# Early root and pre-scaled residual for the last two images, and 64x64 tile products for the first two, in a four-image kernel on one core

## The chip, the cores and the metric

The kernel runs on one core of a Trainium2 chip. The metric is the device time of one execution in microseconds (us); less is better. The core has a matrix engine (TensorE, PE in the tables), a vector engine (VectorE, DVE), a scalar engine (ScalarE, ACT), GpSimd (POOL) and a DMA queue engine (SyncE, SP). Every engine works through its own list of instructions in order and waits on semaphores for the others.

## The reference

Four images of 256 channels and 32x32 pixels pass through four blocks, each of the form x + block(group norm of x). Cut to what the change touches:

```python
def _gn(v, G=32, eps=1e-05): ...            # group norm over 8 channels and all pixels
x = x + _L0(_gn(x), ...)                     # spatial attention, 8 heads
x = x + _L1(_gn(x), ...)                     # selective scan in 4 groups of 64 channels
x = x + _L2(_gn(x), ...)                     # channel attention
x = x + _L3(_gn(x), ...)                     # x + blend of two of seven max pools

# in _L1, for each group g of 64 channels:
dBu = delta * u * Bm                         # Bm: a row of x_dbl = xp_w @ u, spread over the group
h = scan(dA, dBu);  y = h * Cm + Ds * u      # Cm: another such row
y = layernorm(y, og, ob);  out = op_w @ (y * z)
# in _L2:
x_norm = (xt - mean) * rsqrt(var + EPS)      # xt: pixels x channels; one root for each pixel
q, k, v = qkv_w @ x_norm;  attn = softmax(q @ k^T)      # 32 x 32 for each of 8 heads
out = proj_w @ (attn @ v) + proj_b
```

Weights of the scan that belong to one group (`Bm`, `Cm`, `op_w`) are kept on the diagonal of 128x128 matrices, two groups in one, with zeros beside.

## The kernel before

The 256 channels are two chunks of 128 partitions (`cc` or `m`), the 1024 pixels two halves of 512, since a bank of PSUM holds 512 numbers of 4 bytes for each partition. Each image is cut into streams: F (first norm, queries, keys), A (spatial attention), C (its projection, the norm, the convolution of the scan block), B (the scan), D (channel attention), M (max pools of images 0 and 1, summed on VectorE), L and W (max pools of images 2 and 3, summed on TensorE). Every stream is a generator that yields after each step. Four strings (`PE_ORDER`, `ACT_ORDER`, `DVE_ORDER`, `SP_ORDER`) say how many steps of which stream come next on an engine, so the order over the four images is written out by hand; other strings (`BANKS_...`) say in which of eight PSUM banks each step's result lies. A step waits for the steps that it needs and for the last reader of its bank.

Names: `XRES[b % 2]` (XR in the rows) holds the residual x of an image; `U` the input of the scan; `XB`, `XC`, `OPW` the block-diagonal weights for Bm, Cm and op_w; `PVR` the inverse roots of the 1024 pixels as 128x8 numbers; `RB` its copy spread 32 times (in `T1`), `R` the root as one row of 1024 on all partitions, which lies in `HB`; `WE` (in `BUF`) is proj_w, attn and the value weights as one 256x256 matrix, scaled by the group norm; `GM` its means, `CST` = WE @ GM; `BE` the bias; `PA_` is the padded image that the pools read, `QST` the other pool buffer from image 2 on.

Block B on VectorE: `scan` multiplies by Bm from PSUM (L1278, steps dbu), scans (L1284), multiplies by Cm (L1290, steps hc); `gated` multiplies the product with op_w by the gate and the input (L1311, steps xm). On TensorE these are `by_chunk` (L1841) and `gated` (L1876): one 128x128 product of 512 columns for each half.

Block D at its end, for every image: when `WE` is there, TensorE makes `cst`, spreads the root (`spread_rows`, L1976: R0, R1), and multiplies WE with the residual in four products (`project`, L1665: out_m_half). ScalarE copies the root into `R`. VectorE makes two passes over each of the four results (`block3_out`):

```python
dst = (out - CST) * R          # L1396, steps x3a
dst = dst + BE + XRES          # L1401, steps x3, with a running sum for the next norm
```

`dst` lies in `PA_`, so this waits until the pools of the image before have been read. The root goes into `HB`, so its spreading waits for the last pool step of the image before (p6_1). Then come the max pools: L1464 to L1483 for the window of 3, and for each wider window one step along the row (L1495) and one along the column (L1500). For images 2 and 3 TensorE adds the pools (L2075, steps acc0 to acc6); each waits for its pool.

## Time and profile before

| what | value |
|---|---|
| median of 3 runs | 740.16 us (739.38 to 746.61) |
| profiled execution | 742.38 us |
| span in its trace, first to last instruction | 740.5 us |
| TensorE busy | 634.9 us (86%) |
| VectorE busy | 545.4 us (74%) |
| ScalarE busy | 417.8 us (56%) |
| granted TensorE clock, mean | 0.917 |

The profiled execution takes 1.9 us more than its span, which is the work before the first and after the last instruction. Shares are means over the whole span: which engine is full changes along it.

### The profile page before, as it was taken

What the parts mean: (1) busy time and instruction counts of PE and PEld (TensorE: products, weight loads), DVE (VectorE), ACT (ScalarE), POOL (GpSimd) and SP (SyncE); (2) the same over time, 40 slices, a digit from 0 to 9 for tenths busy, and PEclk for the clock granted to TensorE, in tenths of its full rate; (3) what the DMA queues carried; (4) which work ended last, traced back from release to release, by engine and by line L of the source; (5) the groups of instructions that cost most, each with busy time, mean ns of one, the idle gap of its engine ahead of it and who ended that gap; (6) DMA issues with size and microseconds to landing.
All of it is one profiled execution on the core that took longest, in us unless ns stands there. A gap on an engine that the chain in (4) does not pass through costs nothing.

```text
span 740.5 us, 9520 instructions
## 1 busy us (share of the span) xinstructions
PE 634.9 (86%) x3472; PEld 303.2 (41%) x3472; DVE 545.4 (74%) x995; ACT 417.8 (56%) x703; POOL 35.5 (5%) x26
## 2 busy tenths in 40 slices
PE   4769996798999979999998897999759659699687
PEld 3545442343333346353543462344315215465332
DVE  3477249523747466857789899987899998999696
ACT  1304644559778658664866795684667754442321
POOL 3300001000002000000030000100020000000000
PEclk9978997799999997999999988999879969899879
DMA  9240141001001220001000400011000001000101
GB/s 322 86 121 2 58 135 29 3 1 28 31 1 57 58 51 2 2 1 58 0 1 1 107 2 1 1 58 57 0 1 1 1 0 58 0 1 1 57 1 57
DMA packets 15855, 26.88 MB, mean 36 GB/s; under 512 B 3601, under 2 KB 7345, under 8 KB 15682
## 3 DMA queue, kind: packets, MB, share of 16 engines
q1 hardware_dynamic: 12512, 22.80, 10.1%
q10 hardware_dynamic: 3298, 3.48, 1.6%
q8 instruction: 28, 0.46, 0.3%
q14 instruction: 17, 0.14, 0.1%
HBM read 14.09 MB, written 4.19 MB: 25 GB/s over the span
## 4 chain that ended last, share of the span: by engine, by line
PE 62%; DVE 19%; ACT 12%; issue 4%; DMA 1%; ACTq 1%; SPq 0%; DVEq 0%
PE PSB L1665 14%; PE PSB L1795 9%; PE PSB L1776 6%; PE PSB L1686 4%; PE PSB L2075 4%; PE PSB L1699 3%; PE PSB L1809 3%; PE PSB L1741 3%; DVE NEGMAX L1185 3%; PE PSB L1761 3%; PE PSB L1909 2%; PE PSB L1876 2%; PE PSB L1841 2%; ACT PT L656 2%; ACT PS L753 2%
## 5 line engine op out<-in xcount | busy, mean ns | idle before, releaser
L1185 DVE TENSOR_REDUCE NEGMAX<-PSB 128x2 f32<-128x512 f32 x128 | 79.5, 681 | 22.8 <-PE PSB L1741 22.6
L656 ACT ACTIVATE PT<-PSB 128x512 f32<-128x512 f32 x128 | 67.4, 606 | 49.2 <-PE PSB L1761 49.0
L1795 PE MATMUL PSB<-XNP,WTAP 64*64 64x512 f32 x576 | 66.8, 616 | 2.6 <-issue 2.6
L1741 PE MATMUL PSB<-KST,QST 96*128 96x256 f16 x256 | 43.4, 320 | 10.8 <-DMA KST<-KL 7.7
L1761 PE MATMUL PSB<-QST,KST 98*128 98x512 f16 x128 | 38.8, 423 | 7.3 <-DMA QST<-ML 6.0
L1795 PEld LDWEIGHTS PSB<-XNP,WTAP 64*64 64x64 f32 x576 | 22.4, 139 | 45.3 <-issue 45.2
L1500 DVE TENSOR_TENSOR PA_<-HB 128x1024 f32<-128x1024 f32 x32 | 39.1, 1223 | 1.3 <-PE PSB L2075 0.6
L987 POOL TENSOR_TENSOR GA<-GA,PT 128x1024 f32<-128x1024 f32 x8 | 20.2, 2540 | 400.2 <-ACT PT L684 400.2
L1741 PEld LDWEIGHTS PSB<-KST,QST 96*128 96x128 f16 x256 | 25.7, 112 | 30.6 <-DMA KST<-KL 8.2
L720 ACT ACTIVATE U<-PSB 64x512 f32<-64x512 f32 x32 | 26.5, 829 | 20.5 <-PE PSB L1795 19.9
L1776 PE MATMUL PSB<-PT,VT 128*32 128x512 f32 x256 | 35.7, 630 | 1.8 <-issue 0.6
L2075 PE MATMUL PSB<-PA_,PT 128*128 128x512 f32 x64 | 33.2, 660 | 4.3 <-ACT PT L915 3.0
L1776 PE MATMUL PSB<-PT,ONES 128*32 128x512 f32 x256 | 34.4, 607 | 0.0
L1495 DVE TENSOR_TENSOR HB<-PA_ 128x1024 f32<-128x1024 f32 x28 | 34.1, 1219 | 0.2
L1699 PE MATMUL PSB<-XF,WDS 128*128 128x256 f32 x128 | 31.3, 403 | 3.1 <-DVE XF L1100 3.1
L1509 DVE SCALAR_TENSOR_TENSOR ACC<-PA_,COEF,ACC 128x1024 f32<-128x1024 f32 x24 | 32.9, 1371 | 0.4
L1164 DVE SCALAR_TENSOR_TENSOR QL<-PSB,QBS,QH 128x512 f16<-128x512 f32 x16 | 11.6, 746 | 26.1 <-ACT QH L631 26.0
L1665 PE MATMUL PSB<-XF,WQ 128*128 128x512 f32 x64 | 29.7, 597 | 0.0
L1665 PE MATMUL PSB<-GA,WP 128*128 128x512 f32 x64 | 29.5, 600 | 0.0
L1665 PE MATMUL PSB<-XR,BUF 128*128 128x512 f32 x64 | 29.1, 597 | 0.0
L1699 PEld LDWEIGHTS PSB<-XF,WDS 128*128 128x128 f32 x128 | 25.4, 201 | 8.5 <-issue 3.2
L1665 PE MATMUL PSB<-PS,WP 128*128 128x512 f32 x64 | 28.8, 598 | 0.0
(294 smaller groups left out, 1293.8 us busy)
## 6 DMA issues: line engine op xcount, KB each, us to landing
XF<-in_x SPq DMA_DIRECT2D x8, 512.0 KB, 3.8
XR<-in_x SPq DMA_DIRECT2D x4, 1024.0 KB, 4.9
QST<-QH SPq DMA_DIRECT2D x24, 128.0 KB, 2.4
out<-ACC SPq DMA_DIRECT2D x2, 1024.0 KB, 4.2
out<-ACC SPq DMA_DIRECT2D x8, 256.0 KB, 2.0
QST<-QL SPq DMA_DIRECT2D x12, 128.0 KB, 2.5
PS<-in_cw ACTq DMA_DIRECT2D x1, 1152.0 KB
WDS<-in_wds SPq DMA_DIRECT2D x1, 1024.0 KB, 7.0
```

The lines of the kernel that those rows point to most:

```text
L656: e.activation(PROB[:, 4 * kt + j, :], bank("A", b, f"st{g}_{kt}_{j}")[:, :], ACT.Exp)\
L1185: e.tensor_reduce(NEGMAX[:, h, 2 * j:2 * j + 2], bank("A", b, f"s{h}_{j}")[:, :].rearrange("p (t k) -> p t k", t=2), AX.X, ALU.max, negate ...
L1495: e.tensor_tensor(HB[:, 1:1 + H, :], x[:, 1:1 + H, 0:W], x[:, 1:1 + H, 2:2 + W], ALU.max)\
L1500: e.tensor_tensor(y[:, 1:1 + H, 1:1 + W], HB[:, 0:H, :], HB[:, 2:2 + H, :], ALU.max)\
L1509: e.scalar_tensor_tensor(out=acc, in0=interior(PA_, cc), scalar=COEF[:, cc, k:k + 1], in1=acc, op0=ALU.mult, op1=ALU.add).then_inc(*dve_m. ...
L1665: mm = e.matmul(s[:, :], w(cc), src[:, cc, hs(half)], start=(cc == 0), stop=(cc == CC - 1))
L1699: mm = e.matmul(s[:, m * NK:(m + 1) * NK], WDS[:, cc, n % 4, m * P:(m + 1) * P], src, start=(n == 0), stop=(n == 4 * CC - 1))
L1741: mm = e.matmul(s[:, t * NK:(t + 1) * NK], QST[0:96, h, qt * P:(qt + 1) * P], KST[0:96, h, :], start=True, stop=True)
L1761: e.matmul(s[:, :], KST[0:98, h, kt * P:(kt + 1) * P], QST[0:98, h, hs(g % 2)], start=True, stop=True)\
L1776: mm = e.matmul(bank("A", b, f"pv{g}_0", n)[HD * j:HD * j + HD, :], w, PROB[:, 4 * kt + j, :], start=(kt == 0), stop=(kt == 1))
L1795: mm = e.matmul(banks[gi][64 * half:64 * half + 64, :], WTAP[rows, cc, tap(2 * cc + gi, dy, dx), :], XNP[rows, cc, dy + 16 * half:dy + 16 ...
L2075: mm = e.matmul(bank("L", b, f"acc0_{cc}", half)[:, :], DG[:, cc, k, :], POOLED[k % 2][:, cc, 1 + 16 * half:17 + 16 * half, 1:1 + W], star ...
```

## The change

**Products of images 0 and 1.** For images below `BLOCKWISE = 2` the three products with block-diagonal weights (Bm, Cm, op_w) are made as two products of 64x64 for each half, without the zeros. In half 0 the lower 64 channels go to the lower 64 partitions of the bank and the upper to the upper; in half 1 they change places, so that the two halves together use four different quarters of the array. VectorE reads a bank of half 1 in two instructions of 64 partitions each, one for each place.

**Root and residual of images 2 and 3.** The root is spread right after the pixel statistics, into a free part of `QST` (`RL`, `RBL`), ahead of the Gram matrix. VectorE then makes (x - GM) * R for both chunks into `GA0` (steps xr0, xr1) while the attention matrix is still being made. `WE` is multiplied with `GA0`, and one pass on VectorE adds bias and residual (`late_out`). `cst` falls away. For images 0 and 1 the end of block D stays, under names of its own (stream steps E).

All order strings and bank tables are new.

```diff
+BLOCKWISE = 2
+        def halves(b, half):
+            if b >= BLOCKWISE or half == 0:
+                return [(slice(0, P), slice(0, P))]
+            return [(to, of) for to, of, _ in parts()[1:]]
```

VectorE in the scan; hc and xm change in the same way:

```diff
-                    e.tensor_tensor(SQ[:, cc, hs(half)], SQ[:, cc, hs(half)], bank("B", b, f"B{cc}_{half}")[:, :], ALU.mult)\
-                     .then_inc(*dve_b.step(f"dbu{cc}_{half}"))
+                    for to, of in halves(b, half):
+                        op = e.tensor_tensor(SQ[to, cc, hs(half)], SQ[to, cc, hs(half)], bank("B", b, f"B{cc}_{half}")[of, :], ALU.mult)
+                    op.then_inc(*dve_b.step(f"dbu{cc}_{half}"))
```

VectorE, images 2 and 3:

```diff
+            def early_root(b):
+                e.wait_ge(*(pe_a.at(B - 1, "st3_1_3") if b == LATE else pe_g.at(b - 1, "R1")))
+                yield from root_columns(b, RBL)
+            def scaled_residual(b):
+                GM = GN["D"][3]
+                e.wait_ge(*act_g.at(b, "r1"))
+                e.wait_ge(*(act_c.at(B - 1, "xn1") if b == LATE else pe_g.at(b - 1, "out_1_1")))
+                for cc in range(CC):
+                    e.scalar_tensor_tensor(out=GA0[:, cc, :], in0=XRES[b % 2][:, cc, :], scalar=GM[:, cc, 0:1], in1=RL,
+                                           op0=ALU.subtract, op1=ALU.mult).then_inc(*dve_g.step(f"xr{cc}"))
+                    yield
+            def late_out(b):
+                e.wait_ge(*dve_d.at(b, "be"))
+                e.wait_ge(*pools_read(b - 1))
+                for m, half in BLOCKS:
+                    lo = m * (H + 2) + 1 + 16 * half
+                    e.wait_ge(*pe_g.at(b, f"out_{m}_{half}"))
+                    e.scalar_tensor_tensor(out=PA_[:, lo:lo + 16, 1:1 + W],
+                                           in0=bank("G", b, f"out_{m}_{half}")[:, :].rearrange("p (h w) -> p h w", w=W),
+                                           scalar=BE[:, m:m + 1],
+                                           in1=XRES[b % 2][:, m, hs(half)].rearrange("p (h w) -> p h w", w=W),
+                                           op0=ALU.add, op1=ALU.add,
+                                           accum_out=PART["M"][:, m, half:half + 1]).then_inc(*dve_g.step(f"x3_{m}_{half}"))
+                    yield
 ```

TensorE:

```diff
+            def block_product(b, s, w, src, cc, half):
+                if b >= BLOCKWISE:
+                    return e.matmul(s[:, :], w, src[:, cc, hs(half)], start=True, stop=True)
+                for gi in range(2):
+                    at, to = slice(64 * gi, 64 * gi + 64), 64 * (gi ^ half)
+                    mm = e.matmul(s[to:to + 64, :], w[at, at], src[at, cc, hs(half)], start=True, stop=True)
+                return mm
                 yield from pixel_rows(b)
+                if b >= LATE:
+                    yield from spread_rows(b)
                 yield from gram(b)
...
-                yield from spread_rows(b)
-                e.wait_ge(*pools_read(b - 1))
-                yield from project(b, WE, XRES[b % 2], act_d.at(b, "we1"), pe_d, "out_", "D", dve_d, "x3a_")
+                if b >= LATE:
+                    e.wait_ge(*dve_g.at(b, "xr1"))
+                    yield from project(b, WE, GA0, act_d.at(b, "we1"), pe_g, "out_", "G", dve_g, "x3_")
 ```

The last line of `PE_ORDER`, for one of the order strings:

```diff
-L1 D2 L1 D1 L1 D1 L2 D1 L1 D2 L3 D7 L17
+B1 D2 B2 D5 B12 D1 B4 D2 B4 D4 B2 L3 D1 L1 D4 L4 D5 L1 D1 L1 D1 L4 D1 L1 D2 L2 D4 L17
```

TensorE's list in the scan of image 0, from its first products on, before (XB and XC are the weights for Bm and Cm, L1761 to L1776 the attention of image 1):

```order
L1841 MATMUL PSB<-U,XB 128x512 x2
L1841 MATMUL PSB<-U,XC 128x512
L1761 MATMUL PSB<-QST,KST 128x512 x2
L1776 MATMUL PSB<-PT,VT 32x512 x4
L1776 MATMUL PSB<-PT,ONES 32x512 x4
L1761 MATMUL PSB<-QST,KST 128x512 x2
L1841 MATMUL PSB<-U,XC 128x512
L1761 MATMUL PSB<-QST,KST 128x512 x2
L1776 MATMUL PSB<-PT,VT 32x512 x4
L1776 MATMUL PSB<-PT,ONES 32x512 x4
L1841 MATMUL PSB<-U,XB 128x512 x2
```

and now, in the same place:

```order
L1940 MATMUL PSB<-U,XB 64x512 x2
L1851 MATMUL PSB<-QST,KST 128x512
L1940 MATMUL PSB<-U,XB 64x512 x2
L1851 MATMUL PSB<-QST,KST 128x512 x2
L1940 MATMUL PSB<-U,XC 64x512 x4
L1851 MATMUL PSB<-QST,KST 128x512
L1866 MATMUL PSB<-PT,VT 32x512 x4
L1866 MATMUL PSB<-PT,ONES 32x512 x4
L1851 MATMUL PSB<-QST,KST 128x512 x4
L1866 MATMUL PSB<-PT,VT 32x512 x4
L1866 MATMUL PSB<-PT,ONES 32x512 x4
L1940 MATMUL PSB<-U,XB 64x512 x4
```

Four products of 64x512 in one row are two halves side by side; two in a row are one half with other work between it and the next.

TensorE's list at the end of image 3, from the product with the attention weights (WP,AP_) to the last product out (XR,BUF is WE with the residual), before:

```order
L1947 MATMUL PSB<-WP,AP_ 32x256 x8
L2075 MATMUL PSB<-QST,PT 128x512 x2
L1955 MATMUL PSB<-T,W2V 128x256 x4
L1623 MATMUL PSB<-COL,T 128x1 x4
L2075 MATMUL PSB<-QST,PT 128x512 x2
L2075 MATMUL PSB<-PA_,PT 128x512 x4
L1623 MATMUL PSB<-GM_D,BUF 128x1 x4
L1976 MATMUL PSB<-MAT,T 32x128 x32
L1665 MATMUL PSB<-XR,BUF 128x512 x8
```

and now (GA,BUF is WE with the scaled residual):

```order
L2045 MATMUL PSB<-WP,AP_ 32x256 x8
L2184 MATMUL PSB<-QST,PT 128x512 x2
L2053 MATMUL PSB<-T,W2V 128x256 x4
L1713 MATMUL PSB<-COL,T 128x1 x4
L2184 MATMUL PSB<-PA_,PT 128x512 x4
L1755 MATMUL PSB<-GA,BUF 128x512 x8
```

The product cst and the spreading of the root (L1976) have left this place, and one more pool sum (acc5 of chunk 1) is made ahead of WE: the row QST,PT between WP,AP_ and T,W2V was acc5 of chunk 0 and is acc5 of chunk 1 now.

VectorE's list at the same place of image 3, from the attention weights (AP_) to the last pass over the result, before:

```order
L1374 TENSOR_SCALAR AP_<-AEX,ASUM,AFL 128x32 x2
L1495 TENSOR_TENSOR HB<-PA_ 128x1024
L1500 TENSOR_TENSOR QST<-HB 128x32x32
L1495 TENSOR_TENSOR HB<-PA_ 128x1024
L1500 TENSOR_TENSOR QST<-HB 128x32x32
L1495 TENSOR_TENSOR HB<-QST 128x1024
L1500 TENSOR_TENSOR PA_<-HB 128x32x32
L1495 TENSOR_TENSOR HB<-QST 128x1024
L1378 TENSOR_TENSOR BE<-PSB,COL 128x2
L1500 TENSOR_TENSOR PA_<-HB 128x32x32
L1381 COPY T<-PVR 128x256
L1384 COPY CST<-PSB 128x2
```

and now:

```order
L1426 TENSOR_SCALAR AP_<-AEX,ASUM,AFL 128x32 x2
L1586 TENSOR_TENSOR QST<-HB 128x32x32
L1581 TENSOR_TENSOR HB<-QST 128x1024
L1586 TENSOR_TENSOR PA_<-HB 128x32x32
L1581 TENSOR_TENSOR HB<-QST 128x1024
L1430 TENSOR_TENSOR BE<-PSB,COL 128x2
L1586 TENSOR_TENSOR PA_<-HB 128x32x32
L1465 SCALAR_TENSOR_TENSOR PA_,PART_M<-PSB,BE,XR 128x16x32 x4
```

Eight pool steps of image 2 stood behind the attention weights, five stand there now; the other three, the copy of the root and the two instructions xr stand ahead of them.

## Rows read from the trace of the kernel before

**Rows 1.** Stretches: from:to, length, busy us (PE, PEld, DVE, ACT, POOL), clock, DMA.

```profile
185.60:231.40 45.80, 45.21 (x185) 15.92 (x186) 28.61 (x39) 35.38 (x59) 1.62 (x1) 1.00 0.02 9
306.00:343.00 37.00, 35.57 (x259) 16.06 (x257) 26.89 (x54) 22.71 (x45) 0.00 (x0) 1.00 0.05 14
...
412.00:500.00 88.00, 80.35 (x546) 37.94 (x539) 81.38 (x130) 65.08 (x110) 2.02 (x1) 0.92 0.12 32
...
621.40:640.20 18.80, 16.93 (x49) 6.59 (x47) 14.42 (x33) 9.05 (x13) 0.00 (x0) 1.00 0.00 0
640.20:674.80 34.60, 30.65 (x138) 19.51 (x139) 31.52 (x76) 11.90 (x35) 0.00 (x0) 0.85 0.00 1
674.80:698.40 23.60, 21.33 (x138) 11.46 (x137) 16.11 (x24) 6.54 (x12) 0.00 (x0) 1.00 0.12 45
```

**Rows 2.** TensorE in order of time, image 0's scan: start, length, line, records.

```profile
185.63 1.95 PE L1841 MATMUL PSB<-U,XB 128*128 128x512 f32 x4 [0.79 <-ACT PT L656]
187.42 1.02 PE L1841 MATMUL PSB<-U,XC 128*128 128x512 f32 x2
...
217.50 1.09 PE L1809 MATMUL PSB<-SQX,MAT 64*64 64x512 f32 x8
218.52 1.98 PE L1665 MATMUL PSB<-XF,WQ 128*128 128x512 f32 x4
```

**Rows 3.** VectorE in order of time, scans of images 0 and 1; idle before in brackets.

```profile
191.18 2.29 DVE L1284 TENSOR_TENSOR_SCAN PS<-PS,SQX 128x1024 f32<-128x1024 f32 x1 [1.69 <-ACT PS L766]
...
202.14 1.48 DVE L1290 TENSOR_TENSOR PS<-PS,PSB 128x512 f32<-128x512 f32 x2 [1.92 <-PE PSB L1841]
...
325.19 0.69 DVE L1278 TENSOR_TENSOR SQX<-SQX,PSB 128x512 f32<-128x512 f32 x1 [1.74 <-PE PSB L1841]
...
332.22 0.69 DVE L1202 TENSOR_TENSOR GA<-GA,PSB 128x512 f32<-128x512 f32 x1 [6.34 <-ACT GA L669]
```

**Rows 4.** Groups by line: busy us, mean ns of one, idle before.

```profile
L1294 DVE SCALAR_TENSOR_TENSOR U<-U,COL,PS 128x1024 f32<-128x1024 f32 x8 | 10.2, 1280 | 0.1
...
L677 ACT ACTIVATE SQX<-PS 128x1024 f32<-128x1024 f32 x8 | 8.4, 1055 | 14.1 <-DVE PS L1311 14.1
```

**Rows 5.** VectorE in order of time, end of image 2's block D.

```profile
618.05 3.33 DVE L1311 SCALAR_TENSOR_TENSOR PS<-PSB,GS,XNP 128x512 f32<-128x512 f32 x4
622.51 0.75 DVE L1396 SCALAR_TENSOR_TENSOR PA_<-PSB,CST,HB 128x512 f32<-128x512 f32 x1 [1.13 <-PE PSB L1665]
623.30 0.75 DVE L1401 SCALAR_TENSOR_TENSOR PA_<-PA_,BE,XR 128x512 f32<-128x512 f32 x1
...
628.34 0.69 DVE L1144 TENSOR_TENSOR PS<-PSB,PS 64x512 f32<-64x512 f32 x1 [1.82 <-ACT PS L687]
```

**Rows 6.** The chain that ended last, image 3's scan: start, length, engine, tile, line.

```profile
625.74 3.58 PE PSB L1686 x16
629.32 7.06 PE PSB L1665 x16
```

**Rows 7.** VectorE in order of time, end of image 3's block D.

```profile
674.65 1.22 DVE L1495 TENSOR_TENSOR HB<-PA_ 128x1024 f32<-128x1024 f32 x1
675.91 1.23 DVE L1500 TENSOR_TENSOR QST<-HB 128x1024 f32<-128x1024 f32 x1
...
687.85 0.16 DVE L1384 COPY CST<-PSB 128x2 f32<-128x2 f32 x1 [2.96 <-PE PSB L1623]
691.83 0.75 DVE L1396 SCALAR_TENSOR_TENSOR PA_<-PSB,CST,HB 128x512 f32<-128x512 f32 x1 [3.81 <-PE PSB L1665]
```

**Rows 8.** The chain that ended last, end of image 3's block D.

```profile
679.24 1.73 PE PSB L1955 x8
680.97 0.79 PE PSB L1623 x8
681.75 5.28 PE PSB L2075 x12
...
687.82 1.89 PE PSB L1976 x64
689.70 7.08 PE PSB L1665 x16
```

More of the change, by code:

```diff
@@ L107 @@
 PE_D = """
[L108 removed]
+gn2 xnT0 xnT1 xnT2 xnT3 gram0 gram1 gramT T1 A PAT WE be
 """
@@ L116 @@
 ln_var3 pb3 pbi gram0 gram1 ab aok aclip anan amax arow afill arec arok
-ap0 ap1 be rb cst x3a_0_0 x3_0_0 x3a_0_1 x3_0_1 x3a_1_0 x3_1_0 x3a_1_1
-x3_1_1
+ap0 ap1 be
+"""
+PE_E = """
+cst R0 R1 out_0_0 out_0_1 out_1_0 out_1_1
+"""
+ACT_E = """
+r0 r1
+"""
+DVE_E = """
+rb cst x3a_0_0 x3_0_0 x3a_0_1 x3_0_1 x3a_1_0 x3_1_0 x3a_1_1 x3_1_1
+"""
+PE_G = """
+R0 R1 out_0_0 out_0_1 out_1_0 out_1_1
+"""
+ACT_G = """
+r0 r1
+"""
+DVE_G = """
+rb xr0 xr1 x3_0_0 x3_0_1 x3_1_0 x3_1_1
 """
@@ L895, in pool_stats @@
                 e.wait_ge(stored, stores_before(b))
-                yield from squares(b, 3, act, [dve_d.at(b, f"x3_{cc}_1") for cc in range(CC)],
+                yield from squares(b, 3, act, [third(b)[2].at(b, f"x3_{cc}_1") for cc in range(CC)],
                                    lambda cc: interior(PA_, cc), lambda cc: ACC[:, cc, :].rearrange("p (h w) -> p h w", h=H))
@@ L1289, in scan @@
                     e.wait_ge(*pe_b.at(b, f"C{cc}_{half}"))
-                    e.tensor_tensor(PS[:, 2 * cc, hs(half)], PS[:, 2 * cc, hs(half)], bank("B", b, f"C{cc}_{half}")[:, :], ALU.mult)\
-                     .then_inc(*dve_b.step(f"hc{cc}_{half}"))
+                    for to, of in halves(b, half):
+                        op = e.tensor_tensor(PS[to, 2 * cc, hs(half)], PS[to, 2 * cc, hs(half)], bank("B", b, f"C{cc}_{half}")[of, :], ALU.mult)
+                    op.then_inc(*dve_b.step(f"hc{cc}_{half}"))
                     yield
@@ L1875, in gated @@
                         e.wait_ge(*dve_b.at(b, f"yz{cc}"))
-                        e.matmul(s[:, :], OPW[:, cc, :], G[:, cc, hs(half)], start=True, stop=True)\
-                         .then_inc(*pe_b.step(f"op{cc}_{half}"))
+                        block_product(b, s, OPW[:, cc, :], G, cc, half).then_inc(*pe_b.step(f"op{cc}_{half}"))
                         yield
```

202 lines of the change are left out of this document (121 added, 81 removed), and 6 rows, old and new, of the table BANKS_B.

## The prediction, as it stood before the run

> **What bounds the kernel now.** The chain of waits gives TensorE 62% of the end and VectorE 19%, but that is a mean over two stages, so I read the table of stretches next. In the scan of image 0 (first row of [rows 1]) TensorE is busy 45.2 of 45.8 us at the full clock, and VectorE 28.6. In the scan of image 1 (second row) it is 35.6 of 37 against 26.9. From 412 us on the order turns: VectorE is busy 81.4 of 88 us, and it stays so until the end of block D of image 3, with three places where it waits: about 500 us, 621 to 640 (14.4 busy of 18.8) and 675 to 698 (16.1 of 23.6) [rows 1]. After 698 only max pools on VectorE are left, 37 us that the change doesn't touch. So a product on TensorE is worth something in the scans of images 0 and 1, and an instruction of VectorE counts from image 1's end on.
>
> The order of time of VectorE names the two last places. In image 2 it waits 1.13 us for the product out, then 1.82 us for the squares of the second norm [rows 5]. In image 3 it waits 2.96 us for cst and 3.81 us for out [rows 7]; the chain shows why: after WE (679.24) TensorE makes be 0.79, six pool sums 5.28, cst 0.79 (a second row like that of 680.97), the root 1.89 and out 7.08 us, one behind the other [rows 8].
>
> **Products of images 0 and 1, TensorE.** Two full products of 512 columns take 1.79 us, from 185.63 to the next start at 187.42. Four tiles of 64x64, such as the variance products already are, take 1.02 us, from 217.50 to 218.52 [rows 2]. So a pair of halves saves 0.77 us where the two halves stand side by side. By the new order that is so for five pairs of image 0 (C0, B1, C1 and both of op) and two of image 1 (the second half of C0 with the first of B1, and op0): 7 x 0.77 = 5.4 us. The other ten halves stand alone, with other work between. Two tiles then fill half of the array; no row shows that, but they can't take more than four do, so such a half costs between 0 and 1.02 - 0.90 = 0.12 us more than now, at most 1.2 us together. TensorE gives up 4.2 to 5.4 us; I take 4.8.
>
> How much of it reaches the end? All of it, if TensorE alone sets the pace until the pools of image 0 begin (at 341 us); that is the one bound, -4.8. The other is nothing or a little worse, since VectorE's part grows on the same path (next). TensorE is busy 98.7% and 96% in the two scans [rows 1], which is nearer to the first bound, yet its stops there (1.4 us in the second) and VectorE's wait of 6.34 us for the sums of attention [rows 3] don't shrink with it. I take three fifths: **-2.9 us**, bounds -4.8 and +0.7.
>
> **The same products, VectorE.** Each half 1 is now read by two instructions of 64 partitions. An instruction of 64 partitions and 512 columns takes 0.69 us (last row of [rows 5]), as one of 128 does [rows 3]; so each half 1 costs its price once more, 0.69 for dbu and hc and 0.83 for xm (3.33 / 4) [rows 5]. There are six in each image. For image 0 they are hidden: VectorE is idle 17 of 45.8 us there [rows 1], and on the path of the scan itself the waits 1.69 and 1.92 us [rows 3] cover the four of dbu and hc, 2.8 us. Were that cover gone, they would cost these 2.8 and 1.7 for xm. For image 1 dbu and hc (2.8 us) fall where VectorE waits 1.74 and 6.34 us [rows 3] and cost nothing; xm falls after 353 us, where nothing covers it: 2 x 0.83 = **+1.6 us**. The two instructions also give the bank of a half 1 back 0.7 us later; the next reader of such a bank is several products away, so I cost that at nothing.
>
> The Trainium skill has two rules on this, in TensorEngine Tiling (Array Packing). Under PSUM Bottleneck it says that tiles speed up TensorE, not the reading of PSUM; the price above agrees. Under Restrictions and Gotchas it says that different row tiles can't access one bank at the same time; here the two tiles of each half lie in different rows and write one bank. By that rule the pairs would gain nothing. The variance products lie in the same way and take 1.02 us for four [rows 2], so this trace speaks against it; it is a rival below.
>
> **End of image 2.** The new order on VectorE moves six pool steps of image 1 (about 1.25 us each [rows 7], 7.5 together) from ahead of xm to behind it, where VectorE now waits. What is then late next is TensorE: behind the last xm come a square of 1.06 us [rows 4], the sums 3.58 us [rows 6], and eight products of 1.77 us (7.06 / 4 [rows 6]) for proj1 and out, 14.2 us; the last two passes of VectorE add 1.5. That makes 20.3 us where the stretch is 18.8 now [rows 1]. Its own work fits: 14.4 busy, less four passes x3a of 0.79 (623.30 - 622.51 [rows 5]), plus 7.5 is 18.8. Ahead of xm the steps xr come in: 2 instructions over 1024 columns from SBUF, for which the trace has no row; the nearest is the same operation on 128x1024, 1.28 us [rows 4]. With one more operand from SBUF it could be no cheaper than half of it and hardly dearer, so 1.3 to 2.6; I take 2.6. cst (0.2) goes. Sum: +1.5 - 7.5 + 2.6 - 0.2 = **-3.6 us**; -5 if xr and the copy of the root fall into gaps, 0 if the early root holds up the scan (below).
>
> **End of image 3.** From the attention weights on (674.8), by the new order: one pool step 1.26, its sum 1.76 (5.28 / 3 [rows 8]), WE 1.73, be 0.79, four pool products 3.5, out 7.08, one pass 0.83, and 0.2 for hand-overs. That is 17.2 us against 23.6 now: cst, the root and a third of the pool sums are gone from behind WE, and of the four passes x3a only the last one counted, since out at 1.77 us a block is slower than the two passes. But ahead of the attention weights stand now three more pool steps (3.8), xr (2.6) and the copy of the root (0.3): +6.7, of which VectorE's idle time in that stretch, 3.1 us [rows 1], can take a part; I take half. So -6.4 + 6.7 - 1.6 = **-1.3 us**. The bounds are +0.3 (no cover) and -4.1 (all of the cover, and xr at half price). The stall of 2.96 + 3.81 us thus doesn't go: out still comes last, because its eight products stand behind the last pool sums, and these behind the last pool step.
>
> **The sum.** -2.9 + 1.6 - 3.6 - 1.3 = -6.2 us. The profiled execution took 742.38 us, 1.9 of it outside its span, which the change leaves alone: 736.2. It lay 2.2 us above the median of the runs, 740.16, so on the scale of the median I forecast **734.0 us**.
>
> **The rivals.**
> 1. *More of TensorE's gain arrives, and the late images' waits close.* The whole -4.8, image 2 at -5 and image 3 at -4.1, with xm +1.6: -12.3, 728 us. For it: TensorE at 98.7% in image 0's scan. Against: all orders must fit at once.
> 2. *The gain is swallowed.* The root of images 2 and 3 is spread ahead of the Gram matrix: 1.89 us of TensorE and two copies of ScalarE on the path to the scan of image 3, whose softplus chain runs on ScalarE. Then image 2 gives 0, image 3 +0.3, and if the products give only -2, xm takes most of that back: 740 us.
> 3. *VectorE becomes the bound of the scans: slower.* Place: dbu, hc and xm of images 0 and 1. If the new order has filled the gaps that cover them, the ten hidden instructions cost 4 x 0.69 + 2 x 0.83 + 4 x 0.69 = 7.2 us, TensorE waits for y instead of working (its -2.9 is gone), and the rest stays: 734.0 + 7.2 + 2.9 = 744 us. It decides from the point at which less than 2.8 us of idle time is left on either scan's path; there are 3.6 and 8.1 us [rows 3]. If image 2 gives nothing either, 748.
> 4. *The tiles of one bank take turns.* Then the pairs save nothing: 734.0 + 2.9 = 737 us. Rows 2 speak against it.
>
> **How the numbers follow.** Chances: forecast 0.45, rival 1 0.22, rival 2 0.20, rival 3 0.09, rival 4 0.04. About 1% (7.4 us) is what a measurement of this kernel can tell from no change. Faster by over 1% means under 732.8: all of rival 1 and four ninths of the forecast, whose spread is some 4 us to each side: 0.42. Slower by over 1% means over 747.6: two thirds of rival 3: 0.06. Within: 0.52. The range, 725 to 743, holds rivals 1, 2 and 4 and leaves out most of rival 3.
>
> **What would show each step.** Tiles: in image 0's scan the new products appear as rows of 8 records of about 1.0 us; if they take 1.8, rival 4. VectorE: halves 1 in two rows of 0.69, with less idle time than 17 us in that stretch but the scan no later; if the last y of image 0 comes later against the attention of image 1, rival 3. The pools of image 0 should begin 2 to 4 us earlier. Image 2: VectorE nearly without idle time between xm and the last x2, and that stretch about 20 us long. Image 3: from the attention weights to the last pass 17 us, with VectorE still waiting about 7 us in it for out. The prediction is wrong if the stretch from 353 to 618 us, in which I change nothing but xm, comes out several us longer or shorter: the whole order is new there, and a wait that it adds or removes is in no term above.

## The result, and the profile after

The changed kernel is slower: 756.22 us median of 4 runs (754.67 to 758.31), against 741.08 (739.38 to 746.61) for the kernel before in the same session; ratio 1.019, 95% interval 1.014 to 1.024. The forecast was 734, with 725 to 743 as its range. The time before varies by a few us from session to session, so every experiment below has a ratio to runs of the kernel before made beside it.

The page of the changed kernel, its busy times and where its end comes from:

```profile
span 753.9 us, 9588 instructions
...
PE 635.9 (84%) x3504; PEld 294.9 (39%) x3504; DVE 553.9 (73%) x1001; ACT 418.2 (55%) x703; POOL 35.5 (5%) x26
...
PE 63%; DVE 20%; ACT 11%; issue 4%; DMA 1%; ACTq 0%; SPq 0%; DVEq 0%
```

TensorE is busy 1 us longer than before, VectorE 8.5 us longer, and the span is 13.4 us longer: on TensorE nearly all of the loss is waiting. The table of stretches, in the columns of [rows 1], for image 0's scan, then the end of image 2 (it runs beside image 3's scan, from the last xm of that scan to its last x2), from there to image 3's attention weights, and from these to the last pass:

```profile
185.20:240.10 54.90, 47.62 (x220) 15.78 (x220) 37.39 (x49) 40.30 (x66) 4.15 (x2) 0.91 0.00 1
634.60:655.70 21.10, 19.34 (x63) 8.95 (x61) 18.51 (x37) 9.12 (x15) 0.00 (x0) 1.00 0.12 50
655.70:694.10 38.40, 33.85 (x205) 20.81 (x206) 36.66 (x82) 13.21 (x37) 0.00 (x0) 0.87 0.00 1
694.10:712.00 17.90, 17.06 (x63) 8.22 (x61) 9.14 (x15) 5.34 (x10) 0.00 (x0) 1.00 0.16 60
```

Against [rows 1], the last two stretches together are 56.3 us long instead of 58.2, so image 3's end gained. Image 2's end did not: 21.1 instead of 18.8. In image 0's scan TensorE now stands still 7.3 of 54.9 us and its mean clock is 0.91; before it stood still 0.6 of 45.8, at 1.00.

To see where the time goes, one reads when the same step ends in both traces. This table does that for thirteen steps; the first column is the kernel before, in us from the span's start, the others are how much later the step ends. The last four columns are experiments below (no tiles; two repairs of the order; tiles alone and late root alone in the old order).

```
step                         before  changed  e2_order  f2_op_first  e1_tiles  e8_late_out2
image 0 xn (norm of scan)     140.9     +3.0      +3.2         -0.3      +2.2          +1.8
image 0 xm                    232.2     +8.7      +9.6         +2.6      +4.1          +2.9
image 0 x2                    250.9     +9.1     +12.5         +6.3      +4.1          +2.9
image 0 x3                    340.2     +8.9     +10.2         +8.1      +4.8          +1.6
image 1 x2                    401.6     +7.2     +10.4         +5.1      +2.7          +1.6
image 2 convolution           413.0     +6.7      +9.9         +4.6      +2.6           0.0
image 2 v0 (scan)             436.2    +10.8     +12.5         +7.9      +2.6          -1.2
image 2 x2                    525.9    +13.8     +16.8        +10.6      +2.5          +0.3
image 3 xn                    546.6    +13.1     +16.0         +4.9      +2.5          +1.4
image 3 du1 (scan)            588.7    +13.8     +17.4         +8.4      +2.5          +1.7
image 3 x2                    640.2    +15.5     +19.1         +9.4      +2.5          +1.4
image 3 x3                    698.4    +13.6     +17.1         +7.0      +2.5          +0.4
last pool step                735.2    +13.5     +17.0         +6.7      +2.5          +0.5
```

The first 3 us are within what executions of one order differ by at their start (the same old order stands between 0.3 earlier and 4.1 later at 76 us in the experiments). All of the rest is lost by image 2's x2, at 526 us in the kernel before and 540 in the changed kernel, and the late root does nothing until 582.6 us there; behind it the lateness stays between 13 and 16. The prediction had no term for most of that stretch. Three places can be read in the trace.

**Image 0's output products.** TensorE in order of time (start, length, line, records, and in brackets the idle time and what ended it); L1940 are the tiles, L1776 the norm sums of image 1:

```profile
189.39 0.61 PE L1851 MATMUL PSB<-QST,KST 98*128 98x512 f16 x1 [3.07 <-ACT PT L694]
...
199.93 1.09 PE L1940 MATMUL PSB<-U,XB 64*64 64x512 f32 x8
...
229.21 0.94 PE L1776 MATMUL PSB<-GA,MAT 128*64 128x512 f32 x1 [2.08 <-issue]
229.22 1.01 PE L1776 MATMUL PSB<-PT,MAT 128*64 128x512 f32 x1
...
233.97 0.59 PE L1776 MATMUL PSB<-PT,MAT 128*64 128x512 f32 x1
234.50 1.95 PE L1940 MATMUL PSB<-G,OPW 64*64 64x512 f32 x16
```

The pair of tiles takes 1.09 us for eight records, as the variance products of [rows 2] do. But the output products (last row) stand behind image 1's norm sums in TensorE's list. Those start after a stop of 2.08 us, for which the row names no releaser; VectorE's norm of image 1 ends at 228.03 and ScalarE's square of it at 229.12, just ahead of them. They start at half the clock (1.06 us a record, 0.59 from 233.1 on), and the scan's result waits with them. VectorE shows the other side: its xm waits 4.42 us.

```profile
230.46 0.75 DVE L1212 SCALAR_TENSOR_TENSOR QL<-PSB,QBS,QH 128x512 f16<-128x512 f32 x1
235.62 2.30 DVE L1362 SCALAR_TENSOR_TENSOR PS<-PSB,GS,XNP 128x512 f32<-128x512 f32 x3 [4.42 <-PE PSB L1940]
```

TensorE's two other stops in this scan, 3.07 us for ScalarE (first row of its list) and 2.12 us ahead of 220.40, don't show in the result: the input of the output products is ready at 230.54, 2.4 us behind the kernel before and so no later than xn was, and xm ends 8.7 behind.

**Image 2's convolution.** ScalarE issues the copies of image 3's keys for 2.65 us between two read-outs of image 2's convolution, for which TensorE's next product waits 2.66 us; image 3's value product (L1816) then waits 1.37 us more for its bank, which image 1's transposed norm rows hold until ScalarE has read them, and takes 3.78 us at the lower clock (granted 0.50 from 428.5 on) where the kernel before takes 1.99:

```profile
422.59 2.65 ACTq L683 DMA_DIRECT2D KST<-KH  x4
425.29 0.59 ACT L758 ACTIVATE U<-PSB 64x512 f32<-64x512 f32 x1 [2.73 <-issue]
```

```profile
426.03 1.09 PE L1899 MATMUL PSB<-XNP,IPZ 64*64 64x512 f32 x8 [2.66 <-ACT U L758]
428.50 3.78 PE L1816 MATMUL PSB<-WV,XDS 128*128 128x256 f32 x8 [1.37 <-ACT SQX L839]
```

**Image 3's norm, a step four times as long.** VectorE, and below it GpSimd, in order of time:

```profile
543.40 0.69 DVE L1192 TENSOR_TENSOR PT<-PSB,PT 64x512 f32<-64x512 f32 x1
544.02 2.83 DVE L1550 TENSOR_TENSOR PH<-PA_ 128x512 f32<-128x512 f32 x1
546.88 2.72 DVE L1555 TENSOR_TENSOR HB<-PA_,PH 128x512 f32<-128x512 f32 x1
549.52 0.15 DVE L1142 SCALAR_TENSOR_TENSOR GB_D<-GM_D,GR_D 128x2 f32<-128x2 f32 x1
549.59 0.68 DVE L1192 TENSOR_TENSOR PT<-PSB,PT 64x512 f32<-64x512 f32 x1
```

```profile
543.85 5.20 POOL L1035 TENSOR_TENSOR GA<-GA,PT 128x1024 f32<-128x1024 f32 x2 [46.11 <-ACT PT L722]
```

The two rows of L1192 are the variance of image 3's norm, chunk 0 and chunk 1. Between them the new order has two pool steps of image 1, hp_0 and h0_0, which take 0.69 us elsewhere and 2.83 and 2.72 here: they run just while GpSimd adds image 3's two products, and each ends some 0.6 us after one of these has (546.29 and 549.04). In the old order no pool step stands ahead of that variance there.

### The profile page after: what moved, and what is told of

Its sections match the earlier page's. It is cut to its first block, busy times and chain, and to the rows that moved or that the text cites. A ratio compares the mean times of both kernels' runs of the same rounds, so it can differ in the third digit from the quotient of the medians.

```text
span 753.9 us, 9588 instructions
## 1 busy us (share of the span) xinstructions
PE 635.9 (84%) x3504; PEld 294.9 (39%) x3504; DVE 553.9 (73%) x1001; ACT 418.2 (55%) x703; POOL 35.5 (5%) x26
## 4 chain that ended last, share of the span: by engine, by line
PE 63%; DVE 20%; ACT 11%; issue 4%; DMA 1%; ACTq 0%; SPq 0%; DVEq 0%
PE PSB L1755 14%; PE PSB L1885 9%; PE PSB L1866 7%; PE PSB L1776 4%; DVE NEGMAX L1233 4%; PE PSB L1851 4%; PE PSB L2184 4%; PE PSB L1899 3%; PE PSB L1789 3%; PE PSB L1831 2%; PE PSB L1940 2%; DVE HB L1581 2%; PE PSB L1937 2%; PE PSB L2007 2%; ACT PT L694 1%
## 5 line engine op out<-in xcount | busy, mean ns | idle before, releaser
L1885 PE MATMUL PSB<-XNP,WTAP 64*64 64x512 f32 x576 | 64.9, 602 | 0.7 <-issue 0.7
L1851 PE MATMUL PSB<-QST,KST 98*128 98x512 f16 x128 | 40.5, 424 | 10.8 <-DMA QST<-ML 7.0
L1831 PEld LDWEIGHTS PSB<-KST,QST 96*128 96x128 f16 x256 | 23.6, 108 | 33.6 <-DVE NEGMAX L1233 9.9
L1755 PE MATMUL PSB<-GA,WP 128*128 128x512 f32 x64 | 31.6, 633 | 0.3 <-DVE GA L1250 0.3
L1851 PEld LDWEIGHTS PSB<-QST,KST 98*128 98x128 f16 x128 | 12.1, 106 | 44.6 <-issue 13.6
```

The costliest lines, as they stand in the source:

```text
L1755: mm = e.matmul(s[:, :], w(cc), src[:, cc, hs(half)], start=(cc == 0), stop=(cc == CC - 1))
L1831: mm = e.matmul(s[:, t * NK:(t + 1) * NK], QST[0:96, h, qt * P:(qt + 1) * P], KST[0:96, h, :], start=True, stop=True)
L1851: e.matmul(s[:, :], KST[0:98, h, kt * P:(kt + 1) * P], QST[0:98, h, hs(g % 2)], start=True, stop=True)\
L1885: mm = e.matmul(banks[gi][64 * half:64 * half + 64, :], WTAP[rows, cc, tap(2 * cc + gi, dy, dx), :], XNP[rows, cc, dy + 16 * half:dy + 16 ...
```

## The experiments

No run leaves out any part of the computation. Step names: a letter for the stream, the image, and the step (C3:n1_0).

**Tiles alone, in the old order.** The kernel before with `halves` and `block_product` as in the change's diff, nothing else; then the late images' root without tiles in the changed kernel's order:

```diff
 e1_tiles, against the kernel before
+BLOCKWISE = 2        (with halves, block_product)
 e2_order, against the changed kernel
-BLOCKWISE = 2
+BLOCKWISE = 0
```

> The kernel before, its orders and banks untouched, with one addition: the block-diagonal products of images 0 and 1 as 64x64 tiles and VectorE's half 1 in two instructions. Theory 'order' (the loss of 15 us sits in the new order of the steps of images 0 to 2 and its waits, not in either idea): 738 to 743 us, between a gain of 3 and a loss of 2 against before. Rival 'tiles' (VectorE's some 8 us of added instructions, and the banks that come free later for them, make the loss): 748 to 757 us. A gain of 5 or more (736 or less) would say that the tiles are worth what they take off TensorE.

> The changed kernel, its orders and banks untouched, with the tiles switched off (128x128 products again, VectorE's half 1 in one instruction); the late images' early root stays. Theory 'order': 753 to 760 us, as slow as the changed kernel. Rival 'tiles': 741 to 747 us. In the trace, by 'order', the cross terms of image 0 end xm at 238 to 243 us after the span's start as in the changed kernel (232 in the kernel before).

e1_tiles took 745.62 us, ratio 1.004 (1.001 to 1.007): 3 us lost, a little more than 'order' allowed and far from what the tiles would have to lose. e2_order took 759.11, ratio 1.023 (1.016 to 1.030): without its tiles the new order is as slow as with them, or slower; its xm of image 0 ends at 241.8. The rival 'tiles' falls.

**Late root in the old order, first try.** `BLOCKWISE = 0` in the changed kernel, with the orders and banks of the kernel before and the new steps put in by hand; then the same with tiles.

```diff
 VectorE, image 3 (old order, late root)
+D3:pbi G3:rb
 ... D3:arow
+G3:xr0 G3:xr1
 D3:afill D3:arec D3:arok W2:t5_0 ... W2:p6_1 D3:ap0 D3:ap1 D3:be G3:x3_0_0 ...
```

> The kernel before's orders and banks with the late root alone (no tiles): images 2 and 3 spread the root early, the residual is pre-scaled, the constant and the eight read-outs become four; the new steps stand where the trace of before shows room: image 2's root rows behind its attention scores, xr behind the attention weights, three pool steps behind xm; image 3's root rows ahead of the gram, xr behind the last pool step. Theory 'order': 735 to 741 us, a gain of up to 6. Rival 'late root' (the pre-scaled residual and its added waits lose more than the tail gives): 744 us or more. From the kernel before's trace image 3's end should be 2 to 3 us shorter and image 2's stretch from xm to x2 within 1 us of its 18.8.

> The third kernel's orders and banks with the tiles as well: all that the change does to the arithmetic, in the old order. Theory 'order': 733 to 742 us, the sum of the two differences that the first and the third kernel show, within 2 us. If both ideas together cost more than each alone, 745 us or more, the loss of the changed kernel is not its order alone.

e3_late_old took 755.11, 1.017 (1.011 to 1.022), e4_both_old 759.97, 1.024 (1.018 to 1.030), which looks like the rival 'late root'. The trace says otherwise. Up to the gram of image 3 e3_late_old is at most 4.6 us behind; then VectorE, in order of time (L1456 is xr, L1583 and L1588 the pool, L1428 the attention weights):

```profile
677.66 2.47 DVE L1456 SCALAR_TENSOR_TENSOR GA<-XR,GM_D,QST 128x1024 f32<-128x1024 f32 x2
...
689.21 1.23 DVE L1588 TENSOR_TENSOR PA_<-HB 128x1024 f32<-128x1024 f32 x1
690.35 0.50 DVE L1428 TENSOR_SCALAR AP_<-AEX,ASUM,AFL 128x32 f32<-128x32 f32 x2
```

The attention weights came behind the last pool step, 16.1 us later than before. I had put xr ahead of them in the program, so that xr took their places in the order. One misplaced pair of steps cost some 10 us (e5_late_moved, next): a first look at how much a place is worth here.

**Late root in the old order, better placed.** xr behind the bias in both images (e5_late_moved); then image 2's end built for it (e7_late_out, e8_late_out2).

```diff
 e5_late_moved: code of stream D, VectorE
-                if b >= LATE:
-                    yield from scaled_residual(b)
                 yield from channel_softmax(b)
                 yield from attended(b)
+                if b >= LATE:
+                    yield from scaled_residual(b)
 e7_late_out: image 2, TensorE
-D2:be B3:op0_0 ... B3:op1_1 G2:out_0_0 G2:out_0_1 G2:out_1_0 B3:sums2_0 ...
+D2:be G2:out_0_0 G2:out_0_1 B3:op0_0 ... B3:op1_1 G2:out_1_0 B3:sums2_0 ...
 e8_late_out2: image 2, VectorE
-M1:p6_1 M1:acc6_1 G2:x3_0_0 G2:x3_0_1 B3:ln_var2_0 B3:ln_var2
+M1:p6_1 B3:ln_var2_0 M1:acc6_1 B3:ln_var2 G2:x3_0_0 G2:x3_0_1
```

> The late root alone in the old order as in the third kernel (e3_late_old), whose loss of some 12 us its trace puts in one place: there the pre-scaled residual xr of image 3 stood ahead of the last steps of the attention weights in VectorE's stream, so that these came behind the last pool step (attention weights 16.1 us later than before, x3 12.8 later). Here xr stands behind the attention's bias in both images, and nothing else differs. Theory 'place' (the late root costs nothing in itself, where its steps stand decides): 737 to 742 us, some 13 us below the third kernel, image 3's x3 within 2 us of the kernel before's. Rival 'late root' (its longer waits cost wherever it stands): 748 us or more.

> As e5_late_moved, and image 2's end built for it: xr straight behind the attention weights, the first two products out ahead of the scan's output products on TensorE, four pool steps and the four read-outs behind xm on VectorE, the pool's group sums behind x2. If TensorE's queue (output products, out, sums, projection, 1.72 us a product) sets xm to x2, those two products taken out of it give 3 to 4 us: 733 to 739 us. If VectorE's queue sets it, the four pool steps behind xm take the gain back: 738 to 743 us.

> As e7_late_out (no tiles, old order, late root), with the scan's two variance steps on VectorE ahead of the last pool step and of the read-outs: in e7_late_out TensorE's norm sums came 3.4 us earlier than before, the variance step 1.9 and x2 only 1.7, since VectorE was at the pool steps. Expected: image 2's x2 3 to 4 us earlier than before, the end 4 to 5 us earlier, 736 to 739 us. If TensorE's projection or the read-outs set x2: as e7_late_out, 740 to 742 us.

745.91, ratio 1.002 (0.999 to 1.006); 741.55, 0.999 (0.995 to 1.002); 740.74, 0.997 (0.994 to 1.000). So e5_late_moved is 9.2 us below e3_late_old, where 'place' said some 13, and its median is 4 us above what that theory gave; once its neighbours fit the late root gains 4 us at most, by the interval of e8_late_out2, and perhaps nothing. The end of image 2 in e7_late_out, then image 3 to the attention weights, and on to the last pass:

```profile
621.10:638.50 17.40, 13.48 (x41) 5.42 (x39) 16.18 (x33) 8.73 (x12) 0.00 (x0) 1.00 0.15 60
638.50:675.40 36.90, 31.53 (x202) 20.19 (x203) 31.84 (x78) 13.11 (x37) 0.00 (x0) 0.91 0.01 1
675.40:695.70 20.30, 18.76 (x67) 8.76 (x65) 15.14 (x19) 5.34 (x9) 0.00 (x0) 1.00 0.13 52
```

Image 2 gains 1.4 us on its 18.8 in [rows 1], image 3 1.0 on its 58.2. Not all of the first is the late root's: e9_halves (below), in which that stretch is as in the kernel before, takes 17.9 us there. The hoped-for 3 to 4 us in image 2 came in neither e7_late_out nor e8_late_out2: four pool steps behind xm keep VectorE at work for 16.2 of 17.4 us. e8_late_out2 is the only version with an interval below 1; at 0.3% it is no more than a hint.

**Both ideas in the old order.** e8_late_out2 with `BLOCKWISE = 2`.

> Both ideas of the change in the old order and banks: e8_late_out2 with the tiles of e1_tiles switched on. If the two differences add (late root -2, tiles +3 against before): 741 to 746 us, 10 to 15 us below the changed kernel with the same arithmetic, and the order alone makes the loss. If together they lose more than that, 749 us or more, part of the changed kernel's loss is theirs.

743.67, ratio 1.001 (0.998 to 1.003). This is the same arithmetic as the changed kernel, 12.5 us faster than it by medians (13.6 by the two ratios) and as fast as the kernel before: the order and its banks make the loss.

**VectorE's half of the tiles alone.** e1_tiles with TensorE's products whole and the split reads kept:

```diff
-            return [(to, of) for to, of, _ in parts()[1:]]
+            return [(slice(0, 64), slice(0, 64)), (slice(64, P), slice(64, P))]
-                if b >= BLOCKWISE:
+                if b >= 0:
                     return e.matmul(s[:, :], w, src[:, cc, hs(half)], start=True, stop=True)
```

> The kernel before with VectorE's part of the tile idea alone: half 1 of dbu, hc and xm of images 0 and 1 in two instructions over 64 partitions each; TensorE's products stay whole. Some 8 us of instructions are added on VectorE. If VectorE's split is what e1_tiles lost: 744 to 748 us, and TensorE's tiles then give nothing or up to 2 us in this order. If VectorE's waits hide it: 741 to 743 us, and TensorE's tiles themselves, alone or in other places' banks, cost the 3 us.

745.62, ratio 1.004 (1.001 to 1.007), the same as e1_tiles; that they agree to the hundredth is luck, since the intervals leave some 3 us open. The stretches of both scans, in e1_tiles and then in e9_halves, the second from image 1's first product with Bm to its last with op_w (the records differ by the 24 that the tiles add):

```profile
188.00:236.00 48.00, 43.82 (x211) 14.04 (x212) 33.60 (x46) 35.40 (x59) 3.52 (x2) 1.00 0.02 6
309.86:374.50 64.64, 61.01 (x384) 27.17 (x384) 49.51 (x107) 42.37 (x78) 0.00 (x0) 1.00 0.06 18
```

```profile
189.00:237.00 48.00, 46.27 (x187) 16.35 (x188) 33.17 (x46) 35.32 (x59) 3.42 (x2) 1.00 0.01 5
311.04:376.55 65.51, 63.08 (x360) 29.34 (x359) 50.02 (x108) 42.82 (x79) 0.00 (x0) 1.00 0.05 17
```

TensorE gives up 2.45 and 2.07 us with the tiles, and nothing of it shows at the end; VectorE's split costs 2.6 us by the medians, with TensorE's tiles or without. No run has the tiles without the split.

**The new order, part by part.** Kernels in which every step that the kernel before had finished by a given time runs in the old order and banks, the rest in the new:

> The changed kernel with tiles and late root, in which each engine runs the steps that the kernel before had finished by 150 us (setup, image 0's attention, its norms, part of image 1's scores) in the old order and banks, and all others in the new order and banks. By 150 us the changed kernel is 3 to 4 us behind, so if that part of the order costs what it shows there: 751 to 754 us. If the start's delay is taken up by a later wait: 755 to 758 us.

> As h150_old_then_new with the seam at 260 us, so that image 0's scan too runs in the old order, with its tiles. The changed kernel is 7 to 9 us behind there: 746 to 750 us if the loss is the order's. If the tiles made the loss in image 0's scan, 752 us or more, since they stay.

> The changed kernel with all steps that the kernel before had finished by 420 us (images 0 and 1 with their tiles) and the queue of loads in the old order and banks, the rest in the new order. In the two earlier kernels of this kind the loads kept the new order, and VectorE waited 7.15 us for image 2's input at 121.8 us. Theory 'order': what the changed kernel loses up to 420 us (6.7) goes, what it loses behind stays: 748 to 752 us, with 1 to 3 us of uncertainty from banks at the seam. If the tiles or the late root make the loss, the tiles still stand in the first part and the late root in the last: 755 us or more.

785.7 (1.057), 767.67 (1.031) and 758.42 (1.020, interval 1.014 to 1.026): the first two worse than either whole order, the third as slow as the changed kernel. The first two tell nothing of the order, since the seam itself costs: the queue of loads kept the new order, and VectorE waited for image 2's input (h260_old_then_new, VectorE in order of time):

```profile
121.81 1.28 DVE L1094 BATCH_NORM_STATS2 STAT_F<-XF 128x6 f32<-128x512 f32 x2 [7.15 <-DMA XF<-in_x]
```

In h420_loads, whose loads have the old order, image 2's convolution is 1.6 us behind before the seam, and image 2's v0 9.0 behind after it. Part of that is again the seam: TensorE waits 6.9 us there for a bank. So these three bound nothing, but they show that parts of two orders need not fit.

**Repairs of the new order.** f1_norm3 takes image 3's variance and norm out from behind the two long pool steps, f2_op_first adds image 0's output products ahead of image 1's norm sums; both are the changed kernel otherwise, tiles and late root included.

```diff
 f1_norm3: VectorE
-C3:ln_var1_0 M1:hp_0 M1:h0_0 D2:gn_b2 C3:ln_var1 M1:h1_0 D2:g2_0 M1:vp_0 ... D2:ps0 C3:n1_0 C3:n1_1
+C3:ln_var1_0 C3:ln_var1 M1:hp_0 M1:h0_0 D2:gn_b2 M1:h1_0 D2:g2_0 C3:n1_0 C3:n1_1 M1:vp_0 ... D2:ps0
 f2_op_first, with f1's: TensorE
-C1:sums1_0 C1:sums1_1 B0:op0_0 B0:op0_1 B0:op1_0 B0:op1_1
+B0:op0_0 B0:op0_1 B0:op1_0 B0:op1_1 C1:sums1_0 C1:sums1_1
```

> The changed kernel with one repair in VectorE's order: image 3's norm (ln_var1, n1_0, n1_1) ahead of the pool steps hp_0 and h0_0 of image 1, which in the changed kernel's trace take 2.83 and 2.72 us instead of 0.69, because they run while GpSimd adds image 3's two products (543.9 to 549.0 us). Theory 'order': image 3's xn comes some 5 us earlier, and as everything behind it stood 13 to 14 us late, the end does too: 750 to 753 us. If another chain takes its place: 754 to 757 us.

> As f1_norm3, and on TensorE image 0's four output products ahead of image 1's norm sums, which in the changed kernel stand ahead of them and wait for VectorE (the 4.4 us for which VectorE then waits for the output products). Theory 'order': xm of image 0 ends 5 to 7 us earlier, image 1's chain 2 to 4 us earlier: 746 to 751 us. If the lateness is made good or set elsewhere before image 2: within 1 us of f1_norm3.

f1_norm3 took 751.37, ratio 1.012 (1.008 to 1.015), 4.9 us below the changed kernel by medians; the two ratios differ by 0.7%, with some 0.6% of uncertainty. VectorE in its trace:

```profile
541.06 0.69 DVE L1192 TENSOR_TENSOR PT<-PSB,PT 64x512 f32<-64x512 f32 x1 [0.33 <-ACT PT L725]
541.67 1.70 DVE L1550 TENSOR_TENSOR PH<-PA_ 128x512 f32<-128x512 f32 x1
543.41 2.72 DVE L1555 TENSOR_TENSOR HB<-PA_,PH 128x512 f32<-128x512 f32 x1
```

The pool steps are still long (1.70 and 2.72), but the variance no longer stands behind them. Image 3's xn went from 13.1 to 4.7 us behind, of which 3.4 are lateness that this execution didn't have by image 2's xm, ahead of the repair.

f2_op_first took 748.82, 1.009 (1.006 to 1.011). Its repair does what it should: xm of image 0 ends 2.6 us behind instead of 8.3. Most of that is gone at x2 (6.3 against 8.7) and all of it at x3 of image 0 (8.1 against 8.5): image 1's first scan on VectorE starts at 329.6 us (317.5 before, 330.8 in f1_norm3), behind image 0's bias and constant, which the new order puts ahead of it and for which VectorE waits 2.35 and 1.32 us, and behind 2.21 us for ScalarE; the repair left all three. So the trace doesn't show its gain at the end, and the two medians differ by less than their intervals.

**Image 2's convolution.** Three tries, each with the two repairs above. The lines are not all that was moved: f3_conv2 also takes image 2's two gate layers ahead of image 3's scores on TensorE and VectorE, and the expectations tell the rest.

```diff
 f3_conv2: ScalarE
-C2:xd1_0_0 F3:qh1_0 F3:kh0 F3:kh1 (copies) C2:xd1_0_1 ... C2:xd1_1_0 ... C2:xd1_1_1
+C2:xd1_0_0 C2:xd1_0_1 C2:xd1_1_0 C2:xd1_1_1 F3:qh1_0 F3:kh0 F3:kh1 (copies)
 f4_conv_bank, besides: F3:qh1_0 ahead of C2:xd1_0_0; bank of F3:vT
-0
+2
 and VectorE
-M0:acc6_0 M0:hp_1 M0:h0_1 M0:h1_1 F3:vt A3:mx0_0
+F3:vt B2:hm1 A3:mx0_0 ... A3:mx1_3 M0:acc6_0 M0:hp_1 M0:h0_1 M0:h1_1 A3:mx2_0
 f5_conv_pool: those pool steps and three more behind A3:ml0 and D1:gram1
```

> As f2_op_first, and image 2's convolution path: on ScalarE its read-outs ahead of image 3's keys and the 2.65 us of issuing their copies, on TensorE and VectorE the two gate layers ahead of image 3's scores. The changed kernel loses 4 us there (from 6.7 to 10.8 us behind). Theory 'order': another 2 to 4 us, 743 to 748 us, three repairs of a dozen moved rows then giving back two thirds or more of what the change lost. If under 1 us comes of it, that loss belongs to another queue.

> As f2_op_first, and image 2's convolution path repaired by its bank: image 3's value product in the bank that image 2's last convolution product has left, ScalarE's query read-out qh1_0 ahead of the convolution's four read-outs and these ahead of the keys, z0's read-outs ahead of image 1's transposed rows, the gate's two layers right behind z1, image 3's value copy and the gate's step ahead of its row maxima on VectorE. Theory 'bank': image 2's zs and image 3's first scores 3 to 4 us earlier than in f2_op_first (which had 7.6 to 8.0 us against before there), the end 744 to 747 us. If another queue takes over: 748 to 751 us.

> As f4_conv_bank, with seven pool steps of image 0 behind image 3's row maxima and image 1's gram copies on VectorE instead of among them, z1 in banks 6 and 2, and its read-outs behind image 1's transposed rows on ScalarE. Theory 'order': image 2's zs some 4 to 5 us behind the kernel before (8.0 in f2_op_first) and its v0 too, the end 744 to 747 us. If v0 or image 3's scores wait again for something that was moved: 749 us or more, and the place is not repaired by hand.

752.05 (1.012), 754.18 (1.016) and 754.67 (1.019): all worse than without the repair. In each the place that was mended got better and the next one worse. f3_conv2: qh1_0 now came late, VectorE waited 2.8 us for it ahead of image 1's pixel statistics, and the value product waited 4.2 us for its bank. f4_conv_bank: the value product ends at 422.8 us (430.2 in f2_op_first), but the pool steps ahead of image 3's row maxima kept the banks that the Gram product takes (TensorE in order of time, L2007):

```profile
441.00 6.18 PE L2007 MATMUL PSB<-SQX 128*128 128x256 f32 x16 [1.95 <-DVE NEGMAX L1233]
```

f5_conv_pool: v0 6.0 us behind (12.1 in f4_conv_bank), but ScalarE's softplus waits 3.67 us for VectorE's vmin0, which now stands behind seven pool steps:

```profile
453.93 1.06 ACT L795 ACTIVATE PS<-PS 128x1024 f32<-128x1024 f32 x1 [3.67 <-DVE PS L1301]
```

## Why the prediction was wrong

**The step that failed** is the one which it named at its end and costed at nothing: "the whole order is new there, and a wait that it adds or removes is in no term above". It drew that stretch from 353 us; the loss is in it and ahead of it, from the first scan on. The new order and its banks cost 12.5 us (e10_all_old against the changed kernel, the same arithmetic), more than all of the forecast's gains together, of which only that at image 3's end arrived in full. I had looked at the new lists at the three places that the change is about and taken them for neutral elsewhere.

Of those 12.5 us, 4.9 by medians are shown for image 3's norm behind the two long pool steps, with an uncertainty almost as large. For the other two places the wait is shown in the trace, and moving it moves the steps behind it, but no repair brought the end forward beyond doubt. What each is worth at the end stays open.

**Term 1, TensorE's tiles.** The price was about right, where I took 4.8 us: 4.5 given up in both scans in the old order (e1_tiles against e9_halves); in the new one (the changed kernel against e2_order) TensorE is busy 43.9 instead of 48.0 us in image 0's scan, and in image 1's, where eight of twelve halves stand alone, 68.8 instead of 68.4, so nothing. "Three fifths of it reach the end" was not: in the old order nothing shows there (both 745.62, to within some 3 us). I read TensorE's 98.7% as its being the pace; that VectorE's split on the same path takes its place fits these runs, but none shows the tiles without the split. In the new order the tiles may give 3 us (759.11 to 756.22), which the intervals don't settle.

**Term 2, VectorE's halves.** +1.6 was taken, 2.6 measured (e9_halves), and the place was wrong. I had called image 0's hidden and let only image 1's xm count. Between the scan's start in image 0 (lv1) and image 1's v0, e1_tiles and e9_halves lose 1.0 and 1.3 us where e5_late_moved, e7_late_out and e8_late_out2, without the split, gain 1.8, 1.5 and 1.3. So image 0 costs some 2.7; most of image 1's later xm is made good before its x2.

**Term 3, end of image 2: -3.6 predicted, a loss in the changed kernel** (13.8 us behind at image 3's du1, 15.5 at its x2). In e7_late_out it is -1.8 between these two steps, but e9_halves, without the late root, has -1.6 there, so that no gain is shown. The stretch from xm to x2 became 21.1 us, where I had 20.3. The -7.5 is what failed: from y1 to xm image 3's scan takes 19.7 us with the six pool steps gone, 20.3 with them. VectorE was full there, but of work that had time; that the chain of the scan over TensorE and ScalarE sets the stretch is my reading, which no run tests. xr was priced right (1.28 us each; the row that it was taken from, L1294, has as many operands, not one fewer).

**Term 4, end of image 3: -1.3 predicted, -1.9 measured** (15.5 behind at x2, 13.6 at x3). From the attention weights to the last pass 17.9 us against 17.2 forecast, with VectorE waiting for out as foreseen:

```profile
700.78 0.16 DVE L1430 TENSOR_TENSOR BE<-PSB,COL 128x2 f32<-128x2 f32 x1 [1.78 <-PE PSB L1713]
...
706.15 0.75 DVE L1465 SCALAR_TENSOR_TENSOR PA_<-PSB,BE,XR 128x512 f32<-128x512 f32 x1 [4.07 <-PE PSB L1755]
```

**The rivals.** The first two forecast 728 and 740 us, no loss. The third (VectorE becomes the bound of the scans, 744 to 748) had the right sign, and its mechanism, VectorE's added halves, is what e1_tiles and e9_halves show, at 3 us instead of 10. It is not what made the changed kernel slow. The fourth fell: tiles of two rows of the array in one bank took 1.09 us for a pair of halves, where two full products take 1.95 [rows 2]. By the rule of the Trainium skill on it the pairs would have gained nothing (TensorEngine Tiling (Array Packing), Restrictions and Gotchas); the trace does not agree.

## What to carry to other kernels

Where a change brings a new hand-written order, the order is a change of its own: compare the lists over the whole program, not only at the change, and first run the new arithmetic in the old order. A busy share, even 98.7%, doesn't say that an engine sets the pace; take work off it alone, and put work on its neighbour alone, before a fraction is credited. And repairing one wait in a tight order tends to make the next one: an experiment that mends a place has to be read at the place and at the end.
